# Shifted-window attention on one core: the transposed scores of eight heads in one stretch over four PSUM banks, K and Q projections exchanged, the join of the odd half in one instruction

## The chip, the cores and the metric

The kernel runs on one core of one Trainium2 chip. The metric is device time in microseconds (us) from the first to the last instruction of one execution, together with a small fixed part around it. Five engines work side by side, each with its own stream of instructions and joined only by semaphores: TensorE (PE in the profile, its weight loads PEld), VectorE (DVE), ScalarE (ACT), GpSimd (POOL) and SyncE (SP, which issues the DMAs here).

## The reference

The input x has 4 images of 128 channels and 112 x 112 pixels. It is group-normalised (32 groups), projected to Q, K and V, and attended within windows of 7 x 7 tokens of an image rolled by 3 pixels, with 8 heads of 16 channels; the result is added to x. In the lines below q, k and v are of shape [4, 16, 16, 8, 49, 16]: image, window row and column, head, token, channel.

```python
xs = jnp.roll(x, (-3, -3), axis=(-2, -1))
qkv = jnp.einsum('bchw,oc->bohw', xs, w_qkv) + b_qkv[None, :, None, None]
...
scores = jnp.einsum('bxyhqd,bxyhkd->bxyhqk', q, k) * scale
attn = jax.nn.softmax(scores, axis=-1)
out = jnp.einsum('bxyhqk,bxyhkd->bxyhqd', attn, v)
...
x = x + conv_ref(group_norm(x), w_qkv, b_qkv)
```

## The kernel before

A group is 8 windows (half a row of windows, GW = 8, 392 tokens), and there are 128 groups (4 images, 16 bands, 2 halves). Heads stand in pairs: 32 partitions hold the 32 channels of an even and an odd head, so there are HP = 4 head pairs, each on its own 32 rows of the PE array. All engines run a software pipeline with one step per group: in step g the streams hold the later stages of groups g-1 and g-2 and the earlier ones of groups g, g+1 and g+2. The loop body has two steps. The order of work is written out by hand in the `step` function of each engine; semaphores count groups.

Stages of one group, with their lines:

- ACT normalises the pixels to xn (L350), POOL splits xn in two fp16 halves (L273, L275). PE projects K (L697) and Q (L703) of the group into one bank (QK_BANK) with three products each; V (L711, L715) has another bank.
- ACT brings K to SBUF (L357) and POOL splits it (L283, L285). ACT brings Q's high half (L362), DVE makes the low half (L558) and masks it for even and odd heads (`mask_q`, L566, two instructions).
- Row scores (`row_scores`, L730): scores with queries on partitions, in two halves of two head pairs each (j = 0, 1), 48 matmuls a half on tiles of 32 rows x 128 columns. Both halves use banks 0 and 1. DVE takes the negated maximum of each half (L573), so half 1 of PE waits for half 0 of DVE.
- POOL splits the maximum in two bf16 parts (L292, L295), PE turns it (`turn_max`, L737), ACT evacuates it (`evac_neg`, L368).
- Column scores (`column_scores`, L747 and L756): the scores again, with keys on partitions, on tiles of 32 rows x 64 columns (two head pairs by two windows side by side), less the maximum (32 x 128 tiles, `less_maximum`). They come in two halves, u = 0 and 1, both in banks 2 and 3; half 1 waits until ACT's exponential of half 0 (L373) is done.
- After the two exponentials PE sums them over keys (`sum_keys`, L780) and weighs V with them (`weigh`, L794, banks 6 and 7); both work in fp32, so each matmul shows as two records. DVE inverts the sums (L578), ACT and DVE split the inverse (L384, L583), PE spreads it over heads (`spread_inverse`, L806), ACT evacuates the even heads' part (`evac_even`, L390), DVE adds the odd heads' part (`join`, L592, two instructions) and multiplies by the inverse (`scale_rows`, L599). POOL adds the image (L305), SP stores.
- The statistics of the next image (L493) are taken in between on DVE, one block of 448 pixels a step for three of the four images.

The order of a step on PE: sum and weigh (group g-2), project V (g), turn the maximum and column scores half 0 (g-1), row scores half 0 (g), spread (g-2), project K (g+1), column scores half 1 (g-1), row scores half 1 (g), project Q (g+1).

## Time and profile before

| | us |
|---|---|
| three runs | 1022.41, 1020.85, 1024.33 |
| median of the runs | 1022.41 |
| the profiled execution, whole | 1024.01 |
| its span, first to last instruction | 1022.1 |
| PE busy | 967.7 (95%) |
| PEld busy | 764.0 (75%) |
| DVE busy | 793.8 (78%) |
| ACT busy | 696.6 (68%) |
| POOL busy | 596.4 (58%) |

Busy time is the union of the times in which an engine had an instruction under way. Matmuls are pipelined and each record lasts about 0.2 us, so a busy PE is not a PE at its peak; what a stretch of matmuls costs is read from the distance between the starts of one stretch and the next. The granted clock of TensorE is full in all but the first two slices of the span and a few at the edges (mean 0.985).

### The profile page before, as it was taken

What the parts mean: (1) busy time and instruction counts of PE and PEld (TensorE: products, weight loads), DVE (VectorE), ACT (ScalarE), POOL (GpSimd) and SP (SyncE); (2) the same over time, 40 slices, a digit from 0 to 9 for tenths busy, and PEclk for the clock granted to TensorE, in tenths of its full rate; (3) what the DMA queues carried; (4) which work ended last, traced back from release to release, by engine and by line L of the source; (5) the groups of instructions that cost most, each with busy time, mean ns of one, the idle gap of its engine ahead of it and who ended that gap; (6) DMA issues with size and microseconds to landing.
All of it is one profiled execution on the core that took longest, in us unless ns stands there. A gap on an engine that the chain in (4) does not pass through costs nothing. (4 is left out here: it accounts for less than half of the span.)

```text
span 1022.1 us, 104511 instructions
## 1 busy us (share of the span) xinstructions
PE 967.7 (95%) x46595; PEld 764.0 (75%) x46595; DVE 793.8 (78%) x1532; ACT 696.6 (68%) x1297; POOL 596.4 (58%) x1067
## 2 busy tenths in 40 slices
PE   0589999999999999999999999999999999999985
PEld 0367777777778777777778787777778777777764
DVE  6667888888888888888888888888877777777762
ACT  1447777777777777777777777777777777777752
POOL 1345665666666566666656665666666566666641
PEclk9979999999999999999999999999999999999995
DMA  9301101111111111111111000000000000000000
GB/s 381 131 4 63 63 31 63 63 49 45 63 63 33 61 63 57 37 63 63 40 55 47 32 16 31 31 31 16 32 31 16 31 31 31 16 31 31 19 31 35
DMA packets 29920, 51.96 MB, mean 51 GB/s; under 512 B 3650, under 2 KB 28868, under 8 KB 29764
## 3 DMA queue, kind: packets, MB, share of 16 engines
q1 hardware_dynamic: 29892, 51.59, 14.3%
q8 instruction: 17, 0.28, 0.1%
q14 instruction: 11, 0.09, 0.0%
HBM read 25.89 MB, written 25.69 MB: 50 GB/s over the span
## 5 line engine op out<-in xcount | busy, mean ns | idle before, releaser
L573 DVE TENSOR_REDUCE neg_max<-psum 100x16 f32<-100x784 f32 x256 | 249.4, 974 | 159.8 <-PE psum L730 159.8
L373 ACT ACTIVATE probs_t<-psum,exp_scale 128x800 f32<-128x800 f32 x256 | 237.3, 927 | 82.1 <-PE psum L747 52.8
L283 POOL TENSOR_SCALAR k_hi<-k 128x392 f16<-128x392 f32 x128 | 67.8, 530 | 230.2 <-PE psum L747 228.1
L730 PE MATMUL psum<-k_hi,q_masks 32*128 32x49 f16 x8192 | 197.5, 179 | 1.1 <-issue 0.6
L747 PE MATMUL psum<-q_masks,k_hi 32*64 32x100 f16 x8192 | 187.7, 207 | 3.3 <-issue 3.3
L305 POOL TENSOR_TENSOR stage<-mixed,image 128x343 f32 (+7 forms) x256 | 160.9, 650 | 43.5 <-issue 32.3
L730 PEld LDWEIGHTS psum<-k_hi,q_masks 32*128 32x128 f16 x8192 | 174.9, 91 | 10.9 <-issue 0.7
L730 PE MATMUL psum<-k_lo,q_masks 32*128 32x49 f16 x4096 | 182.2, 179 | 0.0
L566 DVE TENSOR_SCALAR q_masks<-q_halves,even_odd 128x800 f16<-128x800 f16 x256 | 171.6, 710 | 0.1
L747 PEld LDWEIGHTS psum<-q_masks,k_hi 32*64 32x64 f16 x8192 | 151.6, 105 | 26.4 <-issue 4.1
L730 PEld LDWEIGHTS psum<-k_lo,q_masks 32*128 32x128 f16 x4096 | 160.6, 91 | 0.0
L747 PE MATMUL psum<-q_masks,k_lo 32*64 32x100 f16 x4096 | 158.4, 204 | 0.0
L350 ACT ACTIVATE xn<-image,shift_c,rstd_c 128x21 f32 (+6 forms) x256 | 131.3, 564 | 8.0 <-DVE shift_c L553 6.1
L780 PEld LDWEIGHTS psum<-probs_t,sum_rows 128*32 128x32 f32 x8192 | 101.3, 111 | 45.2 <-issue 45.1
L794 PE MATMUL psum<-probs_t,v_rows 64*32 64x100 f32 x8192 | 132.0, 254 | 2.2 <-issue 2.2
L285 POOL TENSOR_TENSOR k_lo<-k,k_hi 128x392 f16<-128x392 f32 x128 | 117.2, 916 | 10.7
L275 POOL TENSOR_TENSOR xn_lo<-xn,xn_hi 128x392 f16<-128x392 f32 x128 | 116.4, 909 | 10.7
L780 PE MATMUL psum<-probs_t,sum_rows 128*32 128x49 f32 x8192 | 119.0, 210 | 2.3 <-issue 1.2
L357 ACT ACTIVATE k<-psum,k_bias 128x392 f32<-128x392 f32 x128 | 75.3, 588 | 64.6 <-PE psum L697 64.6
L747 PEld LDWEIGHTS psum<-q_masks,k_lo 32*64 32x64 f16 x4096 | 118.6, 106 | 0.0
L362 ACT ACTIVATE q_halves<-psum,q_bias 128x392 f16<-128x392 f32 x128 | 75.8, 592 | 52.6 <-PE psum L703 52.6
L794 PEld LDWEIGHTS psum<-probs_t,v_rows 64*32 64x32 f32 x8192 | 103.2, 106 | 11.2 <-issue 2.6
(120 smaller groups left out, 1881.8 us busy)
## 6 DMA issues: line engine op xcount, KB each, us to landing
out_dram<-stage SPq DMA_DIRECT2D x64, 224.0 KB, 2.0
out_dram<-stage SPq DMA_DIRECT2D x64, 168.0 KB, 1.9
image<-in_x_dram SPq DMA_DIRECT2D x32, 224.0 KB, 2.6
image<-in_x_dram SPq DMA_DIRECT2D x1, 6104.0 KB, 27.3
image<-in_x_dram SPq DMA_DIRECT2D x34, 168.0 KB, 2.5
image<-in_x_dram SPq DMA_DIRECT2D x6, 896.0 KB, 9.7
image<-in_x_dram SPq DMA_DIRECT2D x1, 728.0 KB, 14.1
w_nat<-in_L_conv_w_qkv_dram SPq DMA_DIRECT2D x1, 192.0 KB, 2.4
```

What stands on the lines that cost most here:

```text
L275: nc.gpsimd.tensor_tensor(xn_lo[:, par, :, 0:TOK], xn[:, :, :], xn_hi[:, par, :, 0:TOK], ALU.subtract).then_inc(x_split, 1)
L285: nc.gpsimd.tensor_tensor(k_lo[:, par, :, 0:TOK], k, k_hi[:, par, :, 0:TOK], ALU.subtract).then_inc(k_split, 1)
L305: last = nc.gpsimd.tensor_tensor(pixel_view(stage[:, bass.ds(st, BAND)], piece), token_view(mixed[:, half, :, :], piece), pixel_view(image ...
L350: last = nc.scalar.activation(token_view(xn, piece), pixel_view(image[:, bass.ds(at, BAND)], piece), ACT.Identity, bias=shift_c[:, 0:1], s ...
L362: nc.scalar.activation(q_halves[:, 0, :, 0:TOK], psum[:, QK_BANK, 0:GT].rearrange("p (w q) -> p w q", q=TOK), ACT.Identity, bias=q_bias[:, ...
L373: nc.scalar.activation(probs_t[:, 2 * u:2 * u + 2, :, :].rearrange("p h a q -> p h (a q)"), psum[:, COL_BANKS, 0:PAIRS * ROWS2], ACT.Exp, ...
L566: last = nc.vector.tensor_scalar(both[:, :, e, :], q_halves[:, :, :, :].rearrange("p l w q -> p (l w) q"), even_odd[:, e:e + 1], None, ALU ...
L573: nc.vector.tensor_reduce(neg_max[:, par, 2 * j:2 * j + 2, :], psum[0:ROWS2, ROW_BANKS, 0:GT] .rearrange("p h (w k) -> p h w k", k=TOK), A ...
L730: last = nc.tensor.matmul(psum[:, ROW_BANKS.start + h - 2 * j, w * TOK:(w + 1) * TOK], q_masks[rows, par, low + w * ROWS2:low + w * ROWS2 ...
L747: last = nc.tensor.matmul(psum[side, COL_BANKS.start + h % 2, a * ROWS2:(a + 1) * ROWS2], k[rows, par, w, :], q_masks[rows, par, low + w * ...
L780: last = nc.tensor.matmul(psum[c * PC:(c + 1) * PC, SUM_BANK, SPARE_SUM], sum_rows[:, a, e, :, :, :].rearrange("p t w s -> p (t w s)"), pr ...
L794: last = nc.tensor.matmul(psum[c * PC:(c + 1) * PC, OUT_BANKS.start + s, a * ROWS2:(a + 1) * ROWS2], v_rows[side, par, a, c * PC:(c + 1) * ...
```

## The change

1. PE: the column scores of a group are one stretch. For each of 4 window pairs and 3 products, eight matmuls stand side by side (four head pairs by two windows), 96 in a row, over four banks (6 and 7 for head pairs 0 and 1, 2 and 3 for pairs 2 and 3); then 16 matmuls take the maximum off, four side by side. There is one semaphore, `col_mm`, for all. Banks 6 and 7 are those of `weigh`, so the stretch also waits for `join_done` of group g-2 (it waited for `exp_done[1]` and `inv_done` before).
2. K and Q change places: Q of the next group is projected in the middle of PE's step and K at its end; the evacuations on ACT, `low_q` on DVE and `split_k` on POOL move with them.
3. The order on PE becomes V (g), sum (g-2), turn (g-1), weigh (g-2), Q (g+1), row scores half 0 (g), spread (g-2), column scores (g-1), row scores half 1 (g), K (g+1). The orders of ACT, DVE and POOL change to match.
4. `weigh` writes its four window pairs at a distance of 128 words instead of 100. With that `join` is one instruction of 392 elements, and the windows in `summed` and in the bank of the inverse (`PLACE`) stand in another order, put right in `scale_rows`.

The first step below is POOL's.

```diff
-        ROW_BANKS, COL_BANKS, OUT_BANKS = slice(0, 2), slice(2, 4), slice(6, 8)
+        ROW_BANKS, COL_BANKS, OUT_BANKS = slice(0, 2), (slice(6, 8), slice(2, 4)), slice(6, 8)
...
+        PLACE = [w // 2 + PAIRS * (w % 2) for w in range(GW)]
...
             def step(g, n, par):
                 if live(g - 1):
                     split_max(g - 1, 1 - par)
+                if live(g):
+                    split_k(g, par)
                 if live(g - 3):
                     add_image(g - 3, n - 2 + par, 1 - par)
                 if live(g + 2):
                     split_x(g + 2, par)
-                if live(g + 1):
-                    split_k(g + 1, 1 - par)
...
             def join(g):
                 dve.wait_ge(even_done, g + 1)
                 wait(dve, mixed_done, g + 1)
-                by_side = summed[:, :, :].rearrange("p (a s) q -> p s a q", s=2)
-                for s in range(2):
...
+                odd = psum[:, OUT_BANKS, :].rearrange("p s (a q) -> p (s a) q", a=PAIRS)[:, :, QP:QP + TOK]
+                last = nc.vector.scalar_tensor_tensor(summed[:, :, :], odd, v_scale[:, 1:2], even_out[:, :, :, :].rearrange("p s a q -> p (s a) q"),
+                                                      ALU.mult, ALU.add)
...
+            def column_scores(g, par):
+                wait(pe, exp_done[1], g)
+                wait(pe, inv_done, g)
+                wait(pe, join_done, g + 1)
                 for a in range(PAIRS):
                     for n, (k, low) in enumerate(((k_hi, 0), (k_lo, 0), (k_hi, Q_LEN))):
                         for s in range(2):
                             w, side = 2 * a + s, slice(PITCH * s, PITCH * (s + 1))
-                            for h in (2 * u, 2 * u + 1):
+                            for h in range(HP):
                                 rows = slice(h * PC, (h + 1) * PC)
...
+                                nc.tensor.matmul(psum[side, COL_BANKS[h // 2].start + h % 2, a * ROWS2:(a + 1) * ROWS2], k[rows, par, w, :],
...
+                pe.wait_ge(neg_ready, g + 1)
                 for a in range(PAIRS):
-                    for h in (2 * u, 2 * u + 1):
+                    for h in range(HP):
...
-                if u == 0:
...
-                else:
-                    pe.wait_ge(exp_done[0], g + 1)
-                    less_maximum(u, True)
-                    last = scores_of_keys(g, par, u, False)
-                last.then_inc(col_mm[u], 1)
+                last.then_inc(col_mm, 1)
```

In the order of the program the change stands on PE as follows, from the end of row scores half 0 to the start of row scores half 1. Before, the spread of the inverse (L806), K (L697), the maximum (L756) and half 1 of the column scores (L747):

```order
L806 MATMUL psum<-inv_rows,pick_head 128x49 [waits v_evac,inv_split]
L697 MATMUL psum<-xn_hi,w_hi 128x392 [waits q_low,x_split]
L697 MATMUL psum<-xn_lo,w_hi 128x392
L697 MATMUL psum<-xn_hi,w_lo 128x392
L756 MATMUL psum<-neg_rows,pick_window 128x100 [waits exp_done_0]
L756 MATMUL psum<-neg_rows,pick_window 128x100 x7
L747 MATMUL psum<-q_masks,k_hi 64x100 x4
L747 MATMUL psum<-q_masks,k_lo 64x100 x4
L730 MATMUL psum<-k_hi,q_masks 128x49 [waits max_done_0]
```

After (L797 is the spread, L753 the column scores, L760 the maximum, L733 the row scores, L698 K):

```order
L797 MATMUL psum<-inv_rows,pick_head 128x49 [waits v_evac,inv_split]
L753 MATMUL psum<-q_masks,k_hi 64x100 [waits join_done,inv_done,exp_done_1]
L753 MATMUL psum<-q_masks,k_hi 64x100 x7
L753 MATMUL psum<-q_masks,k_lo 64x100 x8
L760 MATMUL psum<-neg_rows,pick_window 128x100 [waits neg_ready]
L760 MATMUL psum<-neg_rows,pick_window 128x100 x15
L733 MATMUL psum<-k_hi,q_masks 128x49 [waits max_done_0]
L698 MATMUL psum<-xn_hi,w_hi 128x392 [waits q_low]
```

The two half stretches with an exponential between them have become one stretch, whose first matmul now waits for the join, and K has moved behind row scores half 1. On DVE one step before (after the row scores' second maximum, the first row):

```order
L573 TENSOR_REDUCE neg_max<-psum 100x16 [waits neg_split,row_mm_1]
L558 SCALAR_TENSOR_TENSOR q_halves<-psum,q_bias,q_halves 128x8x49 [waits q_high]
L578 RECIPROCAL inv<-psum 128x49 [waits sum_mm]
L566 TENSOR_SCALAR q_masks<-q_halves,even_odd 128x16x50 [waits col_mm_1,q_low]
L583 SCALAR_TENSOR_TENSOR inv_rows<-inv_hi,low_rows,inv 128x49 [waits inv_mm,inv_high]
L592 SCALAR_TENSOR_TENSOR summed<-psum,v_scale,even_out 128x4x49 [waits mixed_done,even_done]
L592 SCALAR_TENSOR_TENSOR summed<-psum,v_scale,even_out 128x4x49
L573 TENSOR_REDUCE neg_max<-psum 100x16 [waits neg_split,row_mm_0]
L493 BN_STATS stats<-image 128x6
L599 TENSOR_TENSOR mixed<-psum,summed 128x392 [waits add_done,join_done,inv_mm]
```

and after:

```order
L574 TENSOR_REDUCE neg_max<-psum 100x16 [waits neg_split,row_mm_1]
L567 TENSOR_SCALAR q_masks<-q_halves,even_odd 128x16x50 [waits col_mm,q_low]
L579 RECIPROCAL inv<-psum 128x49 [waits sum_mm]
L584 SCALAR_TENSOR_TENSOR inv_rows<-inv_hi,low_rows,inv 128x49 [waits inv_mm,inv_high]
L494 BN_STATS stats<-image 128x6
L591 SCALAR_TENSOR_TENSOR summed<-psum,v_scale,even_out 128x392 [waits mixed_done,even_done]
L574 TENSOR_REDUCE neg_max<-psum 100x16 [waits neg_split,row_mm_0]
L559 SCALAR_TENSOR_TENSOR q_halves<-psum,q_bias,q_halves 128x8x49 [waits q_high]
L599 TENSOR_TENSOR mixed<-psum,summed 128x2x4x49 [waits add_done,join_done,inv_mm]
```

The low half of Q has moved from the head of the step to a place behind the first maximum, the statistics ahead of the join, and the join is one instruction.

## Rows read from the trace of the kernel before

**Rows 1.** The page, part 1: busy us (share of the span) xinstructions.

```profile
PE 967.7 (95%) x46595; PEld 764.0 (75%) x46595; DVE 793.8 (78%) x1532; ACT 696.6 (68%) x1297; POOL 596.4 (58%) x1067
```

**Rows 2.** Line L711 (V's first matmul, one a step), 76.5 to 983.1 us.

```profile
L711 PE MATMUL psum<-bias_rows,ones_rows x123: 389/389/390, 76.9 to 983.0; 128*128 128x512 f16 x123
```

**Rows 3.** Timeline of PE, one step: start us, us, engine, line, operation xcount.

```profile
600.17 0.35 PE L756 MATMUL psum<-neg_rows,pick_window 32*128 32x100 bf16 x8
600.45 0.24 PE L747 MATMUL psum<-q_masks,k_hi 32*64 32x100 f16 x4
...
602.16 0.33 PE L703 MATMUL psum<-xn_hi,w_lo 128*128 128x392 f16 x1
602.42 0.91 PE L780 MATMUL psum<-probs_t,sum_rows 128*32 128x49 f32 x64
603.26 1.02 PE L794 MATMUL psum<-probs_t,v_rows 64*32 64x100 f32 x64
604.21 0.39 PE L711 MATMUL psum<-bias_rows,ones_rows 128*128 128x512 f16 x1
...
605.24 0.24 PE L747 MATMUL psum<-q_masks,k_hi 32*64 32x100 f16 x4
605.31 0.21 PE L747 MATMUL psum<-q_masks,k_lo 32*64 32x100 f16 x4
...
605.71 0.21 PE L747 MATMUL psum<-q_masks,k_lo 32*64 32x100 f16 x4
605.75 0.21 PE L747 MATMUL psum<-q_masks,k_hi 32*64 32x100 f16 x4
605.90 0.35 PE L756 MATMUL psum<-neg_rows,pick_window 32*128 32x100 bf16 x8
606.77 0.37 PE L806 MATMUL psum<-inv_rows,pick_head 128*128 128x49 f16 x8
...
607.33 0.33 PE L697 MATMUL psum<-xn_hi,w_lo 128*128 128x392 f16 x1
607.59 0.30 PE L756 MATMUL psum<-neg_rows,pick_window 32*128 32x100 bf16 x6
```

**Rows 4.** Line L794 (weigh), weight loads from 603.25 to 603.53, 603.64, 603.765 us.

```profile
L794 PEld LDWEIGHTS psum<-probs_t,v_rows x32: 102/106/108, 603.3 to 603.5; 64*32 64x32 f32 x32
...
L794 PEld LDWEIGHTS psum<-probs_t,v_rows x34: 102/106/108, 603.3 to 603.6; 64*32 64x32 f32 x34
...
L794 PEld LDWEIGHTS psum<-probs_t,v_rows x48: 102/106/108, 603.3 to 603.8; 64*32 64x32 f32 x48
```

**Rows 5.** PE's queue: semaphore waits at 613.24 to 613.25, 613.87 to 613.88 us.

```profile
L140 PEldq EVENT_SEMAPHORE  x1: 51/51/51, 613.2 to 613.2; - x1
...
L802 PEldq EVENT_SEMAPHORE  x1: 51/51/51, 613.9 to 613.9; - x1
```

**Rows 6.** Timelines of DVE, ACT and POOL in and around that step.

```profile
601.91 0.97 DVE L573 TENSOR_REDUCE neg_max<-psum 100x16 f32<-100x784 f32 x1 [0.48 <-PE psum L730]
603.15 0.63 DVE L558 SCALAR_TENSOR_TENSOR q_halves<-psum,q_bias,q_halves 128x392 f16<-128x392 f32 x1 [0.26 <-ACT q_halves L362]
...
604.07 1.41 DVE L566 TENSOR_SCALAR q_masks<-q_halves,even_odd 128x800 f16<-128x800 f16 x2
605.40 0.26 DVE L583 SCALAR_TENSOR_TENSOR inv_rows<-inv_hi,low_rows,inv 128x49 f16<-128x49 f16 x1
605.58 0.74 DVE L592 SCALAR_TENSOR_TENSOR summed<-psum,v_scale,even_out 128x196 f32<-128x196 f32 x2
606.89 0.97 DVE L573 TENSOR_REDUCE neg_max<-psum 100x16 f32<-100x784 f32 x1 [0.57 <-PE psum L730]
...
603.01 1.31 ACT L350 ACTIVATE xn<-image,shift_c,rstd_c 128x343 f32 x3
604.31 0.59 ACT L390 ACTIVATE even_out<-psum,v_scale 128x392 f32<-128x392 f32 x1
...
606.29 0.93 ACT L373 ACTIVATE probs_t<-psum,exp_scale 128x800 f32<-128x800 f32 x1 [0.21 <-PE psum L756]
...
603.08 0.22 POOL L292 TENSOR_SCALAR neg_halves<-neg_max 100x32 bf16<-100x32 f32 x1 [0.17 <-DVE neg_max L573]
```

More of the change, by code:

```diff
@@ L653, in _ @@
             work_out_scales()
+            step(-1, -1, 1)
             step(0, 0, 0)
@@ L700, in project_q @@
             def project_q(g, par):
-                pe.wait_ge(k_evac, g + 1)
+                pe.wait_ge(x_split, g + 1)
+                wait(pe, k_evac, g)
                 for n, (w, xs) in enumerate(products):
@@ L724, in row_scores @@
                     pe.wait_ge(k_split, g + 1)
+                    wait(pe, neg_ready, g)
                 wait(pe, max_done[1 - j], g + j)
@@ L744, in scores_of_keys @@
                             w, side = 2 * a + s, slice(PITCH * s, PITCH * (s + 1))
-                            for h in (2 * u, 2 * u + 1):
+                            for h in range(HP):
                                 rows = slice(h * PC, (h + 1) * PC)
-                                last = nc.tensor.matmul(psum[side, COL_BANKS.start + h % 2, a * ROWS2:(a + 1) * ROWS2], k[rows, par, w, :],
-                                                        q_masks[rows, par, low + w * ROWS2:low + (w + 1) * ROWS2],
-                                                        start=first and a == 0 and n == 0, stop=not first and n == 2, skip_group_check=True)
@@ L750, in scores_of_keys @@
-                return last
-            def less_maximum(u, first):
+                                nc.tensor.matmul(psum[side, COL_BANKS[h // 2].start + h % 2, a * ROWS2:(a + 1) * ROWS2], k[rows, par, w, :],
+                                                 q_masks[rows, par, low + w * ROWS2:low + (w + 1) * ROWS2],
+                                                 start=a == 0 and n == 0, stop=False, skip_group_check=True)
+                pe.wait_ge(neg_ready, g + 1)
                 for a in range(PAIRS):
-                    for h in (2 * u, 2 * u + 1):
+                    for h in range(HP):
@@ L755, in less_maximum @@
                         rows = slice(h * PC, (h + 1) * PC)
-                        last = nc.tensor.matmul(psum[:, COL_BANKS.start + h % 2, a * ROWS2:(a + 1) * ROWS2],
+                        last = nc.tensor.matmul(psum[:, COL_BANKS[h // 2].start + h % 2, a * ROWS2:(a + 1) * ROWS2],
                                                 pick_window[rows, 2 * a:2 * a + 2, :].rearrange("p w k -> p (w k)"),
-                                                neg_rows[rows, :], start=first and a == 0, stop=not first, skip_group_check=True)
@@ L759, in less_maximum @@
[L759 to L772 removed]
+                                                neg_rows[rows, :], start=False, stop=True, skip_group_check=True)
@@ L793, in weigh @@
                             side = slice(PITCH * s, PITCH * (s + 1))
-                            last = nc.tensor.matmul(psum[c * PC:(c + 1) * PC, OUT_BANKS.start + s, a * ROWS2:(a + 1) * ROWS2],
+                            last = nc.tensor.matmul(psum[c * PC:(c + 1) * PC, OUT_BANKS.start + s, a * C:a * C + ROWS2],
                                                     v_rows[side, par, a, c * PC:(c + 1) * PC], probs_t[side, c, a, :],
```

76 lines of the change are left out of this document (33 added, 43 removed).

## The prediction, made before the changed kernel had run

> **What bounds the kernel now.** I read the page's first part, then one line that runs once a step, then one step of PE, then the other engines beside it. PE is busy 95% of the span, the next engine, DVE, 78% [rows 1]. Line L711 runs once a step: between 76.9 and 983.0 us it starts 123 times, so a step takes (983.0 - 76.9) / 122 = 7.43 us, with and without the statistics on DVE [rows 2]. That it does not care whether DVE has more to do says that DVE does not set it. In the step [rows 3] the stretches of PE follow each other without a hole: where a stretch seems to start late, 605.75 to 605.90 or 607.33 to 607.59, the array has to empty because the tiles change shape. From the last set of four of L747 (605.75) to the first of L756 (605.90) are 0.15 us, where a set takes 0.044, so a change of shape costs about 0.11 us. PE is the bound, and the step is the sum of its stretches.
>
> **Column scores, eight side by side.** Between 605.31 and 605.71 nine sets of four matmuls start: 0.40 / 9 = 44 ns a set of 100 columns [rows 3]. Before, a step has 12 sets of four in each half and 4 sets of two for the maximum in each half: 32 sets. After, it is 12 sets of eight and 4 sets of four: 16 sets. At an unchanged 44 ns a set the change takes 16 x 0.044 = 0.71 us off. Changes of shape: ten a step before, nine after (the pair from L756 back to L747 goes, the others are exchanged): another 0.11 us off. The work alone would make the step 7.43 - 0.71 - 0.11 = 6.61 us.
>
> **Can eight be fed?** A set of eight in 44 ns wants a matmul with its weight load every 5.5 ns; four wanted one every 11. The trace has one stretch with eight tiles side by side, L794, in fp32 (each matmul two records), so sets there take longer and want less. Its first 32 weight loads go out by 603.53, the 34th by 603.64, and from there 14 go out in 0.12 us, 8.6 ns each [rows 4]. I read that as a queue that holds about 32 pairs of load and matmul, those under way included, and that is filled again at about 8.6 ns a pair. Nothing in the trace shows the pace for fp16 pairs when the queue is dry; the ends are these. Low: no limit at all, 5.5 ns. High: between two semaphore waits that PE's queue takes in order, at 613.24 and 613.87 us, it took in the 48 matmuls of row scores half 0, so a pair costs at most 0.63 / 48 = 13.1 ns [rows 5]. I take 8.6, the one pace that a row shows. Then the first 32 pairs start at full pace (four sets, 0 to 0.13 us). A 33rd comes in when the first is through, its 0.21 us [rows 3] and 0.03 us later, 0.24 us; the other 63 follow at 8.6 ns, so the last starts at 0.24 + 0.54 = 0.78 us instead of 11 x 0.044 + 0.02 = 0.50. That costs 0.28 us. The maximum (four side by side, 11 ns a pair) and the row scores (12.5 ns a pair) want less than 8.6 and lose nothing. **The step becomes 6.61 + 0.28 = 6.89 us.**
>
> **Waits that the new order adds.** I lay PE's stretches out from S, the start of K after row scores half 1, each as long as in [rows 3], with 0.10 more where the shape now changes behind it: K 0.53, V 0.95, sum 0.84, turn 0.19, weigh 0.95, Q 0.62, row scores half 0 0.73, spread 0.30, column scores 0.65 + 0.28, maximum 0.15, row scores half 1 0.70; together 6.89. Against that:
> - The join. Weigh ends at 3.46; the even part takes 0.1 + 0.59 us, the join, one instruction instead of 0.74 us for two, about 0.63 as L558 with as many elements [rows 6]. Done at about 4.9; column scores start at 5.11. Slack 0.2. Behind that wait stand the whole column scores and row scores half 1, so a late join costs its lateness in full.
> - First maximum. It starts 0.12 us after PE's next stretch (606.77 to 606.89) and takes 0.97: 4.81 + 0.12 + 0.97 = 5.90. Row scores half 1 start at 5.11 + 0.93 + 0.15 = 6.19. Slack 0.3, but none if the eight tiles run at full pace.
> - Exponentials. Both now wait for all the column scores. The first starts 0.2 us behind them, they take 0.83 and 0.93 us: 6.19 + 0.2 + 1.76 = 8.15, which is 1.26 of the next step. The sum, which waits for both, starts at 0.53 + 0.95 = 1.48; K and V are what hides them. Slack 0.2. Behind them on ACT K's evacuation comes at 1.2 instead of 0.9; its splits on POOL start when the split of the maximum is through (0.12 + 1.17 + 0.6 = 1.9), end 1.5 us later at 3.4, and row scores half 0 start at 4.08.
> - DVE. From the first maximum (4.93) on: 0.89, low half of Q 0.54, the product 0.47, free at 6.83; the second maximum can start at 7.0. Busy in all 793.8 / 128 - 0.2 = 6.0 us a step.
> So all are hidden, by 0.2 to 0.7 us, and cost nothing at 6.89. If one of the covers fails by 0.1 us the step is 0.1 longer, 12 us in all. The changes on DVE, ACT and POOL themselves (the single join, 0.1 to 0.2 us less) are worth nothing, since PE is the bound. K's and Q's exchange moves 0.53 us across the step and adds none.
>
> **The sum.** 122 steps at 7.43 - 6.89 = 0.54 us are 66 us. The four first and two last steps, with their own waits and a lower clock, I leave as they are: at half the clock 16 sets would give 1.4 us each, the serial exponentials of the last groups take about as much back. The profiled execution took 1024.0 us; after, 958. The median of the three runs shown is 1.6 us lower, 1022.4, so I forecast 956.
>
> **Rivals.**
> - Full pace. The Trainium skill (TensorE: Matmul & The Clock Gate, section "Measured speedup vs the span model") has tiles side by side cost about 4 ns of issue each, so eight would fit in 44 ns. As a mechanism here: the queue never runs dry, and the step is 6.61, then a little more since the first maximum has no slack, 6.65. 122 x 0.78 = 95 us: 927. For it: the four records of a set lie within 0.21 us, so they start almost at once [rows 3]; against it: the dry spell in [rows 4]. Chance 0.18.
> - The pace is slower, or the four row tiles only run two at a time, so that a set of eight takes 88 ns, 11 ns a pair. The column scores then take 12 x 0.088 and save only the 0.18 us of the maximum and 0.11 of the shape: the step is about 7.14, 122 x 0.29 = 35 us: 987; at the upper bound of 13.1 ns, 7.3, 1007. Chance 0.14.
> - A new wait. One of the three chains with 0.2 us of slack is longer than laid out, by 0.1 to 0.3 us beyond its slack (most likely the column scores' exponentials in front of the sum, since ACT has K, three pieces of x and two copies between them): a step of 7.0 to 7.2, 970 to 992. What speaks against it is that ACT and DVE have 0.9 us of idle a step left. Chance 0.14.
> - Slower. PE's queue takes 17.2 ns for a matmul of either type: 2 x 8.6 is what L794 shows for a whole fp32 matmul, and it may be a price for the instruction and not for the record. The column scores then empty the queue: the last of them starts at 0.24 + 63 x 0.0172 = 1.32 us, 0.82 late, and the 64 matmuls behind it take 1.10 us instead of 0.77. The step is 6.61 + 0.82 + 0.33 = 7.76: 122 x 0.33 = 40 us more, 1062. It decides from 15 ns a pair on; [rows 5] allow 13.1, which speaks against it. The Trainium skill (Runtime: NRT & Kernel Launch, section "Instruction fetch mechanics") states a floor of about 20 cycles for an instruction in the sequencer, an estimate of 16.7 ns at 1.2 GHz. By that rule the change would lose, and the trace agrees with it in fp32 alone. Chance 0.05.
> - The forecast, 940 to 968 with its own small errors: 0.49.
>
> **Range and chances.** The forecast, full pace and the new wait hold 0.81; with part of the third case the range is 924 to 992. A measurement of this kernel tells 0.3% (3 us) from no change. Faster by more: 0.92; within: 0.02, where a slow pace and a wait meet; slower: 0.06, the last rival and what I have not seen.
>
> **What would show it.** The distance of the once-a-step line: 6.89. The column scores from first to last start: 0.78 us if the feed is at 8.6 ns, 0.50 at full pace, 1.06 if pairs; within it the first 32 pairs start in 0.13 us and the rest more slowly. The sum's wait for the exponentials, the column scores' wait for the join and row scores half 1's wait for the first maximum should be near zero; each that is not is the third rival. DVE idle in front of the maxima should grow less than the step shrinks. Wrong would be a step above 7.2 or below 6.7.

## The result, and the profile after

| | before | after |
|---|---|---|
| median of the runs | 1021.6 us (4 runs, 1019.0 to 1024.3) | 967.0 us (4 runs, 966.7 to 969.7) |
| profiled execution, and its span | 1024.0 us, 1022.1 us | 967.2 us, 965.3 us |
| ratio after to before | | 0.9471, 95% interval 0.944 to 0.9502 |
| one plain step | 7.43 us | 6.88 us |

The changed kernel is 5.3% faster. The forecast was 956 us with a range of 924 to 992. The length of a step came out as forecast, and eleven microseconds are missing, most of them at a place where the prediction had not looked. Both are read below.

The page of the changed kernel, part 1, answers to [rows 1]:

```profile
PE 897.0 (93%) x46595; PEld 724.3 (75%) x46595; DVE 738.2 (76%) x1404; ACT 656.9 (68%) x1297; POOL 597.7 (62%) x1067
```

The line that runs once a step, L713 now, in a stretch without an image change; it answers to [rows 2] (durations in ns, then first and last start in us):

```profile
L713 PE MATMUL psum<-bias_rows,ones_rows x25: 377/377/377, 509.1 to 674.3; 128*128 128x512 f16 x25
```

(674.3 - 509.1) / 24 = 6.88 us. Timeline of PE over a part of one such step, which answers to [rows 3] (start us, us, engine, line, operation xcount): sum L771, turned maximum L740, weigh L785, Q L705, spread of the inverse L797, column scores L753, less the maximum L760.

```profile
599.58 0.91 PE L771 MATMUL psum<-probs_t,sum_rows 128*32 128x49 f32 x64
600.42 0.22 PE L740 MATMUL psum<-ident,neg_halves 100*128 100x100 bf16 x1
600.57 1.02 PE L785 MATMUL psum<-probs_t,v_rows 64*32 64x100 f32 x64
601.52 0.34 PE L705 MATMUL psum<-xn_hi,w_hi 128*128 128x392 f16 x1
...
602.84 0.37 PE L797 MATMUL psum<-inv_rows,pick_head 128*128 128x49 f16 x8
603.14 0.25 PE L753 MATMUL psum<-q_masks,k_hi 32*64 32x100 f16 x8
603.21 0.23 PE L753 MATMUL psum<-q_masks,k_lo 32*64 32x100 f16 x8
603.25 0.27 PE L753 MATMUL psum<-q_masks,k_hi 32*64 32x100 f16 x16
603.39 0.28 PE L753 MATMUL psum<-q_masks,k_lo 32*64 32x100 f16 x8
...
603.86 0.28 PE L753 MATMUL psum<-q_masks,k_hi 32*64 32x100 f16 x8
604.08 0.35 PE L760 MATMUL psum<-neg_rows,pick_window 32*128 32x100 bf16 x16
```

No row has a wait behind it: the stretches follow each other as they did before. Sets of eight start at 603.14, 603.21 and 603.25 us; the twelfth and last starts at 603.86, nine sets later, 0.068 us a set on the mean. The same stretch one step later, as counts of L753 in windows that open at 610.0 us and close at 610.208, 610.27 and 610.81 (the two lines of each are the matmuls on k_hi and on k_lo):

```profile
L753 PE MATMUL psum<-q_masks,k_hi x24: 202/203/228, 610.0 to 610.2; 32*64 32x100 f16 x24
L753 PE MATMUL psum<-q_masks,k_lo x8: 202/202/203, 610.1 to 610.1; 32*64 32x100 f16 x8
...
L753 PE MATMUL psum<-q_masks,k_hi x64: 202/224/228, 610.0 to 610.8; 32*64 32x100 f16 x64
L753 PE MATMUL psum<-q_masks,k_lo x32: 199/224/224, 610.1 to 610.7; 32*64 32x100 f16 x32
```

By 610.208, 24 + 8 = 32 matmuls have started, and by 610.27 still only 32. The records put the 33rd 0.254 us behind the first, and from there each of the other 63 follows 8.33 ns behind the one before it, to 0.779 us. The Trainium skill (TensorE: Matmul & The Clock Gate, section "Measured speedup vs the span model") gives about 4 ns of issue for a tile. The first 32 agree with it, at 3 to 4 ns within a set; the other 64 do not.

### Where eleven microseconds are missing

In a plain step the forecast's 0.54 us are there, but L713 is not regular everywhere. Between its starts lie 6.88 us in all plain steps, and 8.28, 7.44, 7.29 and 7.81 us in the four steps at each of the three image changes. That is 3.28 us over four plain steps, three times: 9.8 us. Before, these steps were 7.43 us like all the others. Most of the rest of the eleven is in the last subtraction of the forecast: it put the profiled execution at 958, of which 9.2 us are missing, and took off 1.6 more because the median had lain that much below the profiled execution before. In the changed kernel the two are 0.2 us apart. Busy time over the four steps of the first change, then over four plain steps, in the changed kernel (stretch: length, busy us of each engine with its instructions, clock, DMA share, GB/s):

```profile
234.10:264.90 30.80, 27.85 (x1458) 22.36 (x1456) 26.05 (x65) 20.52 (x41) 18.23 (x32) 1.00 0.15 51
...
602.20:629.70 27.50, 27.50 (x1459) 22.29 (x1460) 22.25 (x41) 20.25 (x42) 18.51 (x33) 1.00 0.08 29
```

PE, which has no hole in the plain steps, is idle for 2.95 us of the change. VectorE has 3.8 us more to do there. PE's wait in the first of these steps, what GpSimd does ahead of it, and what VectorE does ahead of that (in brackets the idle time and who ended it):

```profile
237.33 0.22 PE L740 MATMUL psum<-ident,neg_halves 100*128 100x100 bf16 x1 [1.33 <-POOL neg_halves L296]
...
236.38 0.56 POOL L293 TENSOR_SCALAR neg_halves<-neg_max 100x32 bf16<-100x32 f32 x1 [3.29 <-DVE neg_max L574]
237.03 0.25 POOL L296 TENSOR_TENSOR neg_halves<-neg_max,neg_halves 100x32 bf16<-100x32 f32 x1
...
233.47 0.90 DVE L514 BATCH_NORM_AGGREGATE agg<-stats 128x2 f32<-128x168 f32 x1
...
235.00 0.19 DVE L519 TENSOR_REDUCE g_sum<-mean_row 128x8 f32<-128x32 f32 x1
235.22 0.97 DVE L574 TENSOR_REDUCE neg_max<-psum 100x16 f32<-100x784 f32 x1
```

Read from the last lines up: VectorE aggregates the statistics of the next image from 233.47 to 235.19 and only then takes the second maximum. GpSimd splits it, and TensorE, which turns it, has stood still for 1.33 us. In the second and the fourth step the turn waits 0.49 and 0.85 us in the same way. In the third it does not wait; there the spread of the inverse comes 0.08 us late and the column scores wait 0.21 us for the join. VectorE's low half of the inverse takes 1.10 us in that step instead of 0.48 (the first line is that step, the second a plain one), with GpSimd at work beside it:

```profile
253.00 1.10 DVE L584 SCALAR_TENSOR_TENSOR inv_rows<-inv_hi,low_rows,inv 128x49 f16<-128x49 f16 x1 [0.31 <-ACT inv_hi L385]
...
601.33 0.48 DVE L584 SCALAR_TENSOR_TENSOR inv_rows<-inv_hi,low_rows,inv 128x49 f16<-128x49 f16 x1 [0.30 <-ACT inv_hi L385]
```

The work itself is not new in the code. What is new is where VectorE has its idle time. The costly groups of before, then of after (busy us, mean ns | idle time in front of them, and what ended it):

```profile
L573 DVE TENSOR_REDUCE neg_max<-psum 100x16 f32<-100x784 f32 x256 | 249.4, 974 | 159.8 <-PE psum L730 159.8
L566 DVE TENSOR_SCALAR q_masks<-q_halves,even_odd 128x800 f16<-128x800 f16 x256 | 171.6, 710 | 0.1
L578 DVE RECIPROCAL inv<-psum 128x49 f32<-128x49 f32 x128 | 58.8, 460 | 6.3 <-PE psum L780 6.3
```

```profile
L574 DVE TENSOR_REDUCE neg_max<-psum 100x16 f32<-100x784 f32 x256 | 249.5, 974 | 43.1 <-PE psum L733 18.3
L567 DVE TENSOR_SCALAR q_masks<-q_halves,even_odd 128x800 f16<-128x800 f16 x256 | 98.3, 427 | 0.2
L579 DVE RECIPROCAL inv<-psum 128x49 f32<-128x49 f32 x128 | 60.0, 469 | 92.8 <-PE psum L771 92.8
```

Before, VectorE waited 159.8 us in front of the maxima, 1.25 us a step, and most of the work of an image change stands in front of the second one. After, 43.1 us are left in front of the maxima, and 92.8 us stand in front of the reciprocal, where nothing is put. That this move of the idle time is the reason is read from these rows; no run moves it alone. The runs below do show that the four steps no longer follow TensorE: they take 30.8 us in the changed kernel, 30.8 in e1, where a plain step is 0.16 us longer, and 30.8 in e2, where it is 0.04 shorter. Four steps of before were 29.7. So of the 3.28 us about 2.2 (4 x 0.54) are the shorter step, which these four cannot follow, and the other 1.1 a chain that takes longer in the new order than four steps of before did.

### The profile page after: what moved, and what is told of

Same layout as the page of the kernel before. It is cut to its first block, busy times and chain, and to the rows that moved or that the text cites. A ratio compares the mean times of both kernels' runs of the same rounds, so it can differ in the third digit from the quotient of the medians.

```text
span 965.3 us, 104413 instructions
## 1 busy us (share of the span) xinstructions
PE 897.0 (93%) x46595; PEld 724.3 (75%) x46595; DVE 738.2 (76%) x1404; ACT 656.9 (68%) x1297; POOL 597.7 (62%) x1067
## 4 chain that ended last, share of the span: by engine, by line
PE 86%; DVE 8%; issue 4%; POOL 1%; ACT 1%; DMA 0%; POOLq 0%; SPq 0%; DVEq 0%; ACTq 0%
PE psum L733 16%; PE psum L785 12%; PE psum L753 11%; PE psum L771 10%; PE psum L717 8%; PE psum L705 8%; PE psum L698 7%; PE psum L797 4%; PE psum L760 3%; PE psum L713 3%; PE psum L740 2%; DVE neg_max L574 2%; DVE stats L494 2%; DVE q_halves L559 1%; DVE mixed L599 1%
## 5 line engine op out<-in xcount | busy, mean ns | idle before, releaser
L374 ACT ACTIVATE probs_t<-psum,exp_scale 128x800 f32<-128x800 f32 x256 | 223.6, 925 | 177.8 <-PE psum L760 177.8
L574 DVE TENSOR_REDUCE neg_max<-psum 100x16 f32<-100x784 f32 x256 | 249.5, 974 | 43.1 <-PE psum L733 18.3
L293 POOL TENSOR_SCALAR neg_halves<-neg_max 100x32 bf16<-100x32 f32 x128 | 60.5, 473 | 289.9 <-DVE neg_max L574 289.9
L733 PEld LDWEIGHTS psum<-k_hi,q_masks 32*128 32x128 f16 x8192 | 174.7, 91 | 47.6 <-issue 46.4
L733 PE MATMUL psum<-k_hi,q_masks 32*128 32x49 f16 x8192 | 197.4, 179 | 4.5 <-issue 2.7
L733 PE MATMUL psum<-k_lo,q_masks 32*128 32x49 f16 x4096 | 182.2, 179 | 0.0
L733 PEld LDWEIGHTS psum<-k_lo,q_masks 32*128 32x128 f16 x4096 | 160.5, 91 | 0.0
L306 POOL TENSOR_TENSOR stage<-mixed,image 128x343 f32 (+7 forms) x256 | 144.7, 586 | 10.7 <-DVE mixed L599 7.2
L753 PE MATMUL psum<-q_masks,k_hi 32*64 32x100 f16 x8192 | 129.1, 219 | 6.1 <-issue 3.5
L785 PE MATMUL psum<-probs_t,v_rows 64*32 64x100 f32 x8192 | 132.1, 254 | 1.7 <-issue 1.7
L579 DVE RECIPROCAL inv<-psum 128x49 f32<-128x49 f32 x128 | 60.0, 469 | 92.8 <-PE psum L771 92.8
L286 POOL TENSOR_TENSOR k_lo<-k,k_hi 128x392 f16<-128x392 f32 x128 | 116.5, 910 | 10.7
L771 PE MATMUL psum<-probs_t,sum_rows 128*32 128x49 f32 x8192 | 119.1, 210 | 3.0 <-ACT probs_t L374 3.0
L771 PEld LDWEIGHTS psum<-probs_t,sum_rows 128*32 128x32 f32 x8192 | 101.5, 112 | 16.6 <-ACT probs_t L374 3.3
L753 PE MATMUL psum<-q_masks,k_lo 32*64 32x100 f16 x4096 | 111.5, 218 | 1.7 <-issue 1.7
L753 PEld LDWEIGHTS psum<-q_masks,k_hi 32*64 32x64 f16 x8192 | 103.4, 102 | 11.8 <-issue 6.8
L785 PEld LDWEIGHTS psum<-probs_t,v_rows 64*32 64x32 f32 x8192 | 103.2, 106 | 9.1 <-issue 1.9
L591 DVE SCALAR_TENSOR_TENSOR summed<-psum,v_scale,even_out 128x392 f32<-128x392 f32 x128 | 78.8, 616 | 26.5 <-ACT even_out L391 26.5
L567 DVE TENSOR_SCALAR q_masks<-q_halves,even_odd 128x800 f16<-128x800 f16 x256 | 98.3, 427 | 0.2
L717 PE MATMUL psum<-w_lo,xn_hi 128*128 128x128 f16 x512 | 94.7, 222 | 0.7 <-issue 0.7
```

The lines of the kernel that those rows point to most:

```text
L286: nc.gpsimd.tensor_tensor(k_lo[:, par, :, 0:TOK], k, k_hi[:, par, :, 0:TOK], ALU.subtract).then_inc(k_split, 1)
L306: last = nc.gpsimd.tensor_tensor(pixel_view(stage[:, bass.ds(st, BAND)], piece), token_view(mixed[:, half, :, :], piece), pixel_view(image ...
L374: nc.scalar.activation(probs_t[:, 2 * u:2 * u + 2, :, :].rearrange("p h a q -> p h (a q)"), psum[:, COL_BANKS[u], 0:PAIRS * ROWS2], ACT.Ex ...
L567: last = nc.vector.tensor_scalar(both[:, :, e, :], q_halves[:, :, :, :].rearrange("p l w q -> p (l w) q"), even_odd[:, e:e + 1], None, ALU ...
L574: nc.vector.tensor_reduce(neg_max[:, par, 2 * j:2 * j + 2, :], psum[0:ROWS2, ROW_BANKS, 0:GT] .rearrange("p h (w k) -> p h w k", k=TOK), A ...
L717: last = nc.tensor.matmul(psum[:, V_BANK, a * C:(a + 1) * C], xs[:, par, 2 * a:2 * a + 2, :].rearrange("p w k -> p (w k)"), wv[:, 2, :], s ...
```

## The experiments

Eleven kernels. Each starts from the changed kernel. The plain step is that of the once-a-step line between 506 and 676 us, last start less first over the number of steps between them. Each ratio is to runs of the kernel before that were made beside it (medians from 1019.7 to 1021.6 us); e1 has two runs, e2 one, the others four or five.

| kernel | median us | ratio to before, 95% | plain step us |
|---|---|---|---|
| changed kernel | 967.0 | 0.9471 (0.944 to 0.9502) | 6.883 |
| e1_four | 988.0 | 0.9685 (0.9661 to 0.9708) | 7.05 |
| e2_half_columns | 962.6, one run | | 6.84 |
| e3_image_change | 969.6 | 0.9512 (0.9488 to 0.9537) | 6.89 |
| e4_two_joins | 970.0 | 0.9513 (0.949 to 0.9535) | 6.89 |
| e5_turn | 1064.1 | 1.0421 (1.0399 to 1.0443) | 7.7 |
| e6_turn_spread | 1038.9 | 1.0169 (1.0136 to 1.0203) | 7.5 |
| e7_all | 1038.0 | 1.0172 (1.0151 to 1.0192) | 7.5 |
| e8_turn_free | 955.9 | 0.9371 (0.9345 to 0.9398) | 6.78 |
| e9_turn_spread_free | 999.4 | 0.9795 (0.9764 to 0.9826) | 7.14 |
| e10_change_left_out | 959.0 | 0.9393 (0.9364 to 0.9423) | 6.88 |
| e11_k_split_first | 991.0 | 0.9708 (0.9688 to 0.9728) | 7.07 |

### What eight side by side are worth: e1_four

```diff
-                for a in range(PAIRS):
...
-                            for h in range(HP):
...
+                for u in range(2):
+                    for a in range(PAIRS):
...
+                                for h in (2 * u, 2 * u + 1):
```

> The changed kernel, but the 96 column scores run as 48 of head pairs 0 and 1 and then 48 of pairs 2 and 3, four tiles side by side as before the change; all else is as changed. A: the queue of PE takes in a pair of load and matmul every 8.4 ns, and with four side by side the array wants one every 11 ns, so the feed is no limit: 24 sets of 44 ns, first to last start 23 x 0.044 + 0.01 = 1.03 us instead of 0.78. The step is 6.88 + 0.25 = 7.13 us, in all about 967 + 31 = 998 us. Rival B, that the gain came from the merged stretch and the new order and eight tiles give nothing: within 5 us of 967.

Measured: 988.0 us. Eight beside each other are worth 0.16 us a step, 21 us in all, of 54.6. The other 0.38 us of the step belong to the rest of the change; the prediction had 0.29 of them (0.18 for the maximum four side by side instead of two, 0.11 for one change of tile shape fewer), and no run takes these two apart; 0.07 more is the overlap seen below. The 0.16 is less than the 0.25 expected, and the timeline of PE shows where most of the difference is:

```profile
606.66 0.24 PE L754 MATMUL psum<-q_masks,k_hi 32*64 32x100 f16 x4
...
607.18 0.20 PE L754 MATMUL psum<-q_masks,k_hi 32*64 32x100 f16 x2
607.18 0.20 PE L754 MATMUL psum<-q_masks,k_lo 32*64 32x100 f16 x1
...
607.20 0.28 PE L754 MATMUL psum<-q_masks,k_hi 32*64 32x100 f16 x8
...
607.59 0.24 PE L754 MATMUL psum<-q_masks,k_hi 32*64 32x100 f16 x4
607.76 0.35 PE L761 MATMUL psum<-neg_rows,pick_window 32*128 32x100 bf16 x16
```

At 607.18 the second two head pairs take over, on tiles that the first two do not use. I read the quick change there between matmuls on k_hi and on k_lo as both running for a moment. From the first start to the first of L761 the stretch takes 1.10 us, where 24 sets of 44 ns and a change of shape (0.11) would be 1.17, and that of the changed kernel (603.14 to 604.08) takes 0.94.

### Feed or array: e2_half_columns

```diff
-                                nc.tensor.matmul(psum[side, COL_BANKS[h // 2].start + h % 2, a * ROWS2:(a + 1) * ROWS2], k[rows, par, w, :],
-                                                 q_masks[rows, par, low + w * ROWS2:low + (w + 1) * ROWS2],
+                                nc.tensor.matmul(psum[side, COL_BANKS[h // 2].start + h % 2, a * ROWS2 + QP:(a + 1) * ROWS2], k[rows, par, w, :],
+                                                 q_masks[rows, par, low + w * ROWS2 + QP:low + (w + 1) * ROWS2],
```

> The column scores of the even heads are left out: each of the 96 matmuls streams 50 columns instead of 100, to eight tiles as in the changed kernel; the number of instructions is the same. A, the feed of 8.4 ns a pair sets the stretch once the first 32 are through: the first 32 start in about 0.07 instead of 0.16 us (sets of 25 ns), but the 33rd waits until the first is complete and the other 63 come 8.4 ns apart; first to last start is 0.74 to 0.76 instead of 0.78 us, the step 6.86 us. Rival B, the array or PSUM itself is slower with eight tiles over four banks (64 to 67 ns for a set of 100 columns): with half the columns the stretch falls to about 0.4 us and the step to 6.5 us, some 45 us less in all.

Measured: a step of 6.84 us. The timeline of PE, first and last set of eight and what follows:

```profile
605.28 0.23 PE L753 MATMUL psum<-q_masks,k_hi 32*64 32x50 f16 x8
...
605.98 0.26 PE L753 MATMUL psum<-q_masks,k_hi 32*64 32x50 f16 x8
606.18 0.36 PE L760 MATMUL psum<-neg_rows,pick_window 32*128 32x100 bf16 x16
```

The stretch takes 0.90 us instead of 0.94 with half the columns. The records put the 33rd matmul 0.233 us behind the first and the last 0.758, again 8.33 ns a pair. So neither the array's columns nor what is written to PSUM sets the pace; it is that at which load and matmul pairs arrive. Nor is it the loading of weights as such: the loads have the same form throughout, and the ninth to the 32nd of them start 3.6 ns apart in e2. The full-pace rival, and the one in which row tiles run two at a time, are both out.

### The single join: e4_two_joins

```diff
-                last = nc.vector.scalar_tensor_tensor(summed[:, :, :], odd, v_scale[:, 1:2], even_out[:, :, :, :].rearrange("p s a q -> p (s a) q"),
-                                                      ALU.mult, ALU.add)
+                for s in range(2):
+                    half = slice(s * PAIRS, (s + 1) * PAIRS)
+                    last = nc.vector.scalar_tensor_tensor(summed[:, half, :], odd[:, half, :], v_scale[:, 1:2], even_out[:, s, :, :], ALU.mult, ALU.add)
```

> The changed kernel with the join of the odd half in two instructions of 196 elements, as before the change, about 0.13 us more on VectorE a step and in front of the column scores. A, the join has 0.2 us of slack and PE is the bound: step 6.88, 967 us, within 2 us. Rival B, the join is on the path already: up to 0.13 us a step, 6.95 to 7.01, 975 to 983 us.

Measured: 970.0 us, a step of 6.89; its interval and that of the changed kernel overlap. In the plain step the single join is worth nothing that can be told, as the prediction had it: a join 0.13 us longer (0.74 in [rows 6] against 0.61) stands under 0.2 us of slack. The total is 3 us up where A had at most 2, and far from B's 975. There is one place where the longer join shows: the third step of each image change takes 7.41 us instead of 7.29, the step in which the column scores wait for the join. Three times 0.12 are 0.4 us.

### The image change: e10_change_left_out and e3_image_change

```diff
-                step(2 * n, n, 0, after=lambda: gather_channels(b))
-                step(2 * n + 1, n, 1, after=group_variance)
-                step(2 * n + 2, n + 1, 0, first=guess_root, after=lambda: refine_root(1))
-                step(2 * n + 3, n + 1, 1, first=lambda: refine_root(NEWTON - 2), after=lambda: offer(b))
+                step(2 * n, n, 0)
+                step(2 * n + 1, n, 1)
+                step(2 * n + 2, n + 1, 0)
+                step(2 * n + 3, n + 1, 1, after=lambda: offer(b))
```

(and `offer` keeps only its last instruction for b above 0)

> The changed kernel, in which VectorE's work at an image change is left out (aggregation, group variance, root and hand-out; only the last instruction, which gives the signal, stays, so that images 1 to 3 are normalised with image 0's numbers). Theory A (this work in front of the second maximum is the whole of the missing time): the twelve steps of the three changes fall to 6.88, total 966.97 - 9.85 = 957.1, range 955.5 to 959. Rival B (the changes are long for another cause, the load of the next image or ScalarE's wait for the new numbers): at least 3 us of the 9.85 stay, 960 or more.

Measured: 959.0 us, 8.0 less by the ratios. The once-a-step line over the four steps of the first change:

```profile
L714 PE MATMUL psum<-bias_rows,ones_rows x6: 377/377/377, 226.4 to 260.8; 128*128 128x512 f16 x6
```

(260.8 - 226.4) / 5 = 6.88: all twelve steps are plain ones now. Theory A holds; of the 9.8 us that this gives, the last interval of the once-a-step line, 11.3 us instead of 9.8, takes 1.5 back. In it TensorE's granted clock falls to 0.5 (1.2 GHz, the lower of its two levels) for the last 2.9 us, in the changed kernel for the last 0.8; whether that is all of the 1.5 is not shown.

e3 keeps the work and moves it to where VectorE is idle now:

```diff
+                if hole:
+                    hole()
                 if live(g - 2):
                     invert(g - 2)
...
+                if gap:
+                    gap()
                 if live(g - 2):
                     join(g - 2)
...
+                step(2 * n, n, 0, hole=lambda: aggregate(b), gap=gather_groups)
+                step(2 * n + 1, n, 1, hole=squares, gap=sum_squares)
+                step(2 * n + 2, n + 1, 0, hole=guess_root, gap=lambda: refine_root(1))
+                step(2 * n + 3, n + 1, 1, hole=lambda: refine_root(NEWTON - 1), gap=lambda: hand_out(b))
```

> The changed kernel, with the work of an image change on VectorE (means, variances and roots of the next image, in four steps for each of three images) moved from in front of the second maximum, and from the head of the step, to two places where VectorE waits anyway: behind the two masks (it waits 0.7 us for the sum there) and in front of the join (0.4 us). A, this work in front of the maximum is what makes 12 steps 7.3 to 8.3 instead of 6.88 us long, 9.8 us in all: these steps fall to 6.9 to 7.1, the time to 958 to 959 us. Rival B, the steps are longer for another reason (the first group of an image on ScalarE, statistics, a load): they stay above 7.3 us, and the time is 965 or more.

Measured: 969.6 us, no gain; by its own numbers this run would speak for B, and it is e10 that decides for A. The steps of the first change are 7.04, 7.30, 7.56 and 8.65 us: the first is mended (8.28 in the changed kernel), the last two are worse. At the second and third change the fourth step takes 9.78 and 9.56 us. That of the second change, on VectorE and then on PE:

```profile
473.98 0.17 DVE L552 TENSOR_TENSOR rs_t<-rs 128x8 f32<-128x8 f32 x1
...
474.59 0.38 DVE L552 TENSOR_TENSOR rs_t<-rs 128x8 f32<-128x8 f32 x1
475.00 0.17 DVE L553 SCALAR_TENSOR_TENSOR rs_t<-rs_t,g_var 128x8 f32<-128x8 f32 x1
475.21 0.77 DVE L554 SCALAR_TENSOR_TENSOR rs<-rs_t,rs 128x8 f32<-128x8 f32 x1
476.01 0.47 DVE L597 RECIPROCAL inv<-psum 128x49 f32<-128x49 f32 x1
...
477.19 0.20 PE L749 MATMUL psum<-k_hi,q_masks 32*128 32x49 f16 x2 [0.76 <-ACT neg_rows L369]
...
479.13 0.25 PE L769 MATMUL psum<-q_masks,k_hi 32*64 32x100 f16 x8 [0.77 <-DVE summed L609]
```

Two things happen. Two instructions that take 0.17 us elsewhere take 0.38 and 0.77 here. They end at 474.97 and 475.98, where GpSimd, which is splitting K beside them, ends its high half (474.96) and its low half (475.96). And the reciprocal is late, ScalarE's copy of it stands ahead of the copy of the turned maximum, so row scores wait 0.76 us; the hand-out in front of the join costs the column scores another 0.77.

### Turning the maximum later: e5 to e9 and e11

The chain that ends late at a change ends at the turned maximum. These kernels move it behind weigh and Q, into bank 4, with ScalarE's copies in the order even, V, maximum, Q (V, even, maximum, Q in e6, e7 and e9).

```diff
-                if live(g - 1):
-                    turn_max(g - 1)
                 if live(g - 2):
                     weigh(g - 2, par)
                 if live(g + 1):
                     project_q(g + 1, 1 - par)
+                if live(g - 1):
+                    turn_max(g - 1)
```

> The changed kernel, with the turned maximum written to the bank of K and Q and made right behind the projection of Q, which has the same tile shape, instead of between the sum and weigh. Of nine changes of shape on PE a step eight are left. A, the step is the sum of PE's stretches and a change of shape costs 0.11 us: step 6.77, time 967 - 122 x 0.11 = 954 us. Rival B, another chain takes over at once (the first maximum in front of the second half of the row scores, or the exponentials in front of the sum): the step falls by less than half of that, 960 or more.

Measured: 1064.1 us, a step of 7.7, far off. I had left row scores half 0 with their wait for the copy of the turned maximum, which before had shared their bank. In the view of waits (us in total, times, longest), and on PE, ScalarE and PE again in one step:

```profile
PE psum L733 <- ACT neg_rows L369: 102.3, 120, 1.3
```

```profile
605.91 0.21 PE L742 MATMUL psum<-ident,neg_halves 100*128 100x100 bf16 x1
...
606.44 0.26 ACT L369 CAST neg_rows<-psum 128x100 bf16<-128x100 f32 x1
...
606.95 0.20 PE L733 MATMUL psum<-k_hi,q_masks 32*128 32x49 f16 x2 [0.83 <-ACT neg_rows L369]
```

The copy starts only at 606.44, behind the even part and V. e6 (also the spread behind the turn, V's copy first) and e7 (e6 with e3's places) carry the same wait.

> As the kernel with the turned maximum behind Q, and the inverse is spread right behind it too, in front of the first half of the row scores; ScalarE evacuates V before the even part. Seven changes of shape a step are left. A, another 0.11 us off: step 6.66, 940 us. Rival B: the first maximum now has only the column scores to hide behind (1.2 us for 0.12 + 0.97 + 0.06), and the join comes 0.2 us later for V's evacuation: the step stays at 6.70 to 6.80 and the waits in front of column scores or of row scores half 1 show it.

> The two moves on PE and the image change's work in VectorE's idle places together. If the three are independent: 940 - 9 = 931 us. If VectorE has become the bound by then, the moved work costs again and the time is 935 to 945 us.

Measured: 1038.9 and 1038.0 us, a step of 7.5 in both. The wait for the copy of the turned maximum comes in 117 and 125 steps (43.0 and 46.8 us in all), and the spread, now ahead of row scores half 0, waits besides for ScalarE's copy of V, 22.1 us in 121 steps and 23.2 in 125. So neither answers its own question. e8 is e5 without it (bank 0 does not hold the turned maximum any more):

```diff
                     pe.wait_ge(k_split, g + 1)
-                    wait(pe, neg_ready, g)
```

> The earlier run of this order (turned maximum behind Q, into bank 4) kept row scores half 0 waiting for ScalarE's copy of the turned maximum, 1.3 us each step, though bank 0 no longer holds it; that wait is taken out here, nothing else. Theory A (the turn is the end of a chain that misses by 1.33, 0.49 us at each image change, and its change of tile shape between sum and weigh costs TensorE time each step): step 6.77 (6.883 less the 0.11 of one change of shape), the four steps of an image change no longer than 7.3 each, total 966.97 - 14 - 6 = 947, range 938 to 955. Rival B (the column scores' end, which needs the copy, becomes the wait: copy behind even and v on ScalarE): step 6.9 to 7.1, 965 to 985.

Measured: 955.9 us, 0.9371 of before, with its interval (0.9345 to 0.9398) wholly below that of the changed kernel: **e8 is the fastest of all, by some 10 us.** The step is 6.78, as A has it. In the changed kernel the starts of sum, turn and weigh lie 0.84 and 0.15 us apart, and Q to the row scores 0.62; in e8 sum to weigh takes 0.84, Q to turn 0.52 and turn to row scores 0.14. That is 1.61 against 1.50 us, 0.10 for one change of tile shape fewer. The total is just above A's range of 938 to 955, for the part of A on the image changes falls: the four steps of the first change are still 8.10, 7.37, 7.27 and 7.63 us (the first of the second change is 9.21). PE in the first of them:

```profile
233.43 0.21 PE L741 MATMUL psum<-ident,neg_halves 100*128 100x100 bf16 x1
234.89 0.20 PE L732 MATMUL psum<-k_hi,q_masks 32*128 32x49 f16 x2 [1.25 <-issue]
```

The turn is in time now. Row scores start 1.25 us late, 0.1 us behind the low half of K on GpSimd (233.89, 0.91 us), which stands behind the split of the maximum. The same late maximum reaches TensorE by another way.

> The same, with the spread of the inverse ahead of row scores half 0 (so behind the turn, both 128 wide) and ScalarE's copy of V ahead of the even part. A: step 6.66 (two changes of shape fewer), 925 to 942. B: the spread now waits for the inverse's halves or for V's copy, or the even part comes later and the join with it: step 6.8 to 7.1, 955 to 985. I hold B for the likelier by 6 to 4.

Measured: 999.4 us, 7.14 a step: the wait that B names, at a price above B's range (7.1 and 985). The spread waits for the low half of the inverse in nearly every step:

```profile
PEld psum L798 <- DVE inv_rows L584: 58.4, 126, 1.4
```

e11 takes GpSimd's order up: K ahead of the maximum.

```diff
+                if live(g):
+                    split_k(g, par)
                 if live(g - 1):
                     split_max(g - 1, 1 - par)
-                if live(g):
-                    split_k(g, par)
```

> e8_turn_free, in which GpSimd splits K ahead of the maximum (two calls of its step exchanged). In e8 the steps of an image change are still 8.10, 7.37, 7.27 and 7.63 us, and there row scores half 0 start 0.1 us behind K's low half on GpSimd, which stands behind the split of the late second maximum. Theory A (the late maximum reaches TensorE through GpSimd's order, first by the turn, then by K's halves): with K first the late maximum meets only the turn's slack; the change costs 1 to 2 us over four plain steps instead of 3.26, what VectorE's own work then wants, 4 to 6 us off in all: 950 to 952 beside e8's 955.9. Rival B (VectorE itself is full at the change, whatever GpSimd does): the change stays at 3 us or more. Rival C: the split of the maximum now ends at the turn's own place (606.95 against 606.88 in e8's numbers), so every step grows by 0.05 to 0.15, 6 to 18 us, and the kernel ends at 956 to 970.

Measured: 991.0 us, rival C and more: 0.29 us each step where C had at most 0.15. The view of waits:

```profile
PEld psum L741 <- POOL neg_halves L296: 70.3, 121, 2.2
POOL k_hi L284 <- ACT k L358: 299.6, 128, 7.8
```

GpSimd now idles until ScalarE has evacuated K and only then comes to the maximum, which was there earlier, and the turn waits for it in 121 steps. The four steps of the first change are no better either (8.19, 8.02, 7.23 and 7.76 us). How much of e8's 3.3 us is VectorE's own work, and how much its way through GpSimd, stays open; that it is VectorE's work that starts it, e10 shows for the changed kernel.

## The prediction, step by step

- **PE is the bound and a step is the sum of its stretches: right.** No stretch of the plain step has a wait in front of it.
- **16 sets of 44 ns and one change of shape, 7.43 to 6.61: right in sum, so far as it can be told.** In the records column scores and maximum took 1.78 us a step, now 1.13, and the spread in front of them grew by 0.09 since the shape changes there.
- **The feed: right, and the point that carried the forecast.** Forecast 32 pairs, the 33rd at 0.24 us, then 8.6 ns a pair, the last at 0.78. Measured 32, 0.254, 8.33 ns and 0.779. Only the first 32 took 0.18 us instead of 0.13, the second set being 0.07 us behind the first, as it was before (605.24 and 605.31 in [rows 3]). e2 shows it is the feed. That the pace of the fp32 records would hold for fp16 pairs no row had shown, as the prediction said; that it did is in part luck.
- **Covers: right in the plain step.** The column scores start at 603.14 behind the spread, the row scores half 1 and the sum as laid out, each without a wait. The step is 6.883 where the sum gave 6.89. In the third step of each image change the cover of the join does fail, by 0.21 us.
- **"122 steps at 0.54": the step that failed.** It gives 66.3 us. In the traces 109 of the 122 steps gave 0.543 us each, 59.2. The twelve of the image changes gave 0.543 less 0.82 each (3.28 / 4), a loss of 3.3 in all. The first of the 122 took 8.47 us instead of 7.43 and lost 1.0. That makes 54.9. The prediction had read in [rows 2] that the statistics on VectorE leave the step alone and took VectorE's load as its mean, 6.0 us of 6.89. It did not look at the four steps in which 1.7 us stand in front of the second maximum, and did not ask where VectorE's idle time would be after K and Q had changed places. "All hidden" was true for the plain steps.
- **VectorE's load** was put at 6.0 us a step and is 738.2 / 128 = 5.8. The masks alone got 73 us cheaper in all (98.3 against 171.6), which was not foreseen and brought nothing, since VectorE does not set the plain step.
- **Rivals.** Full pace and both slower paces fell with the 8.33 ns; the last rival's 17.2 ns for one instruction stand against 8.33 for two, a load and a matmul. The estimate of 16.7 ns an instruction beside that rival does not hold for these pairs either. The new wait did come, though only in twelve steps. In nine of them it is another chain than the three named, the turned maximum; in the other three it is the join.
- **First and last steps** left as they are: nearly right, on balance. The profiled executions differ by 56.8 us, so all that lies outside the 122 steps gave 2.0.

## What to carry to other kernels

A mean step hides the few steps in which an engine off the path has extra work. Before forecasting a shorter step, list such steps, and lay their extra work into the idle time of that engine as it will lie after the change, not as it lies now: idle time in front of another instruction is no cover by itself, and work moved into it can fail too (e3). When a value moves to another bank or place in the order, go through every wait that stood for the old place: one left over turned a gain of 10 us into a loss of 97 (e5 against e8).

## What the runs showed of the hardware

- A long row of small matmuls with their weight loads is fed at 8.33 ns a pair once 32 pairs are out, whether they have 100 or 50 columns. Eight tiles of 100 columns side by side then run at 67 ns a set of eight (8 x 8.33), not 44; four side by side (e1) stay at 44.
- A change of tile shape on PE costs about 0.10 us here: 6.883 against 6.780 us a step between the changed kernel and e8, which has one fewer.
- VectorE's masks (L566 before, L567 after, 128x800 in fp16) take 427 ns on the mean instead of 710, with the same code. The 710 are a mean of two kinds. Of the 256 before, 135 take less than 0.5 us and 120 more than 0.8. What sets them apart is how long GpSimd's add of the image (L305) still runs when they start:

```profile
603.93 0.98 POOL L305 TENSOR_TENSOR stage<-mixed,image 128x392 f32 x1 [0.31 <-issue]
```

  It ends at 604.91. The first mask of [rows 6] starts at 604.07 and ends at 605.14, 0.23 us behind it. 185 masks start while L305 is under way, and 177 of them end 0.22 to 0.24 us behind its end, however early they start; of the 71 others none takes more than 0.43. In the changed kernel the add stands at another place in the step, and 249 of the 256 masks take about 0.42.
- The same shows for other pairs. Of the 116 low halves of the inverse (L584) that start while GpSimd makes K's low half (L286), 113 end 0.05 to 0.08 us behind its end. In e3 the instructions of 0.38 and 0.77 us end up to 0.02 us behind GpSimd's, and L553, at 0.17 us, starts in a gap between two of them. The other way round, GpSimd's copy of the maximum's halves (L293) takes 473 ns on the mean where it took 218 (L292 before), and mostly ends 0.07 us behind the second mask. Not every pair does so: the reciprocal (L579), which reads PSUM, keeps its 0.47 us with GpSimd at work. What decides it is not shown.
